# VectorE's finishing of a group, moved one slot later and put between the sum and the cast of h

## What is computed

```python
h = x                                            # relu(layernorm(x)) of the layer
for l in range(5):
    m = jnp.einsum('bnd,de->bne', h, weight[l])
    agg = jnp.einsum('bij,bid->bjd', A, m)       # A = (adj != 0)
    gi, gh = agg @ w_ih.T + b_ih, h @ w_hh.T + b_hh
    r = sigmoid(gi_r + gh_r)
    z = sigmoid(gi_z + gh_z)
    n = tanh(gi_n + r * gh_n)
    h = (1 - z) * n + z * h
out = x + h * mask[..., None]
```

## Time and profile before

| | |
|---|---|
| median of 3 runs | 686.35 us (685.84 to 688.16) |
| the profiled execution's own time | 686.79 us |
| its span, first to last instruction | 684.7 us |
| busy: PE / DVE / ACT / POOL | 95% / 87% / 77% / 60% of the span |
| gated layer, first slots | from about 300 us |
| gated layer, finishing inside the rounds | 420 to 660 us |

### The profile page before, as it was taken

How to read it: one execution, slowest core, us unless ns; L and a number is a source line. 1 busy time by engine, 2 the same in 40 slices (tenths; PEclk the granted TensorE clock), 3 DMA queues, 4 the chain that set the end, 5 groups by cost and what they waited for, 6 DMA issues and landing times. The chain is left out here.

```text
span 684.7 us, 13204 instructions
## 1 busy us (share of the span) xinstructions
PE 652.9 (95%) x4380; PEld 424.8 (62%) x4380; DVE 594.9 (87%) x1349; ACT 526.3 (77%) x964; POOL 410.2 (60%) x367
## 2 busy tenths in 40 slices
PE   4899999999999999989999999999999999999995
PEld 3678888888888888865555444545555555555452
DVE  3877787777778877888999899999999999999995
ACT  3688888888888888867687787777877777877774
POOL 4556676677666666464774755555555555555554
PEclk9999999999999999999999999999999999999997
DMA  6111111111000110012232333333333343333532
GB/s 159 32 33 32 32 32 32 32 32 34 22 19 24 32 32 17 10 24 47 51 59 49 59 63 74 67 78 70 69 62 65 76 79 77 61 64 78 78 74 66
DMA packets 114691, 35.82 MB, mean 52 GB/s; under 512 B 87681, under 2 KB 114625, under 8 KB 114625
## 3 DMA queue, kind: packets, MB, share of 16 engines
q1 hardware_dynamic: 113424, 34.79, 23.9%
q10 hardware_dynamic: 1200, 0.20, 0.2%
HBM read 9.80 MB, written 4.19 MB: 20 GB/s over the span
## 5 line engine op out<-in xcount | busy, mean ns | idle before, releaser
L1553 POOL TENSOR_TENSOR h0T<-r,zh 128x512 f32<-128x512 f32 x80 | 104.1, 1302 | 140.4 <-DVE r L1587 140.2
L52 PE MATMUL psum<-t_parts,gru_w 128*128 128x512 f16 x720 | 181.7, 379 | 6.2 <-DVE t_parts L1577 6.2
L52 PE MATMUL psum<-h_parts,gru_w 128*128 128x512 f16 x720 | 181.8, 379 | 2.1 <-DVE r L1591 1.2
L52 PEld LDWEIGHTS psum<-h_parts,gru_w 128*128 128x128 f16 x720 | 69.7, 98 | 83.6 <-DVE r L1591 5.3
L52 PEld LDWEIGHTS psum<-t_parts,gru_w 128*128 128x128 f16 x720 | 65.4, 98 | 77.0 <-DVE t_parts L1577 15.5
L1547 POOL TENSOR_TENSOR zh<-z,h0T 128x512 f32<-128x512 f32 x80 | 102.7, 1284 | 15.0 <-ACT z L1525 14.7
L1522 ACT CAST t_parts<-psum 128x512 f16<-128x512 f32 x80 | 46.8, 585 | 60.9 <-PE psum L52 60.6
L1435 DVE CAST h_parts<-h0T 128x512 f16<-128x512 f32 x80 | 84.0, 1050 | 2.0 <-POOL h0T L1553 1.9
L691 POOL TENSOR_TENSOR prob<-prob,row_max 128x512 f32<-128x512 f32 x64 | 68.7, 1086 | 22.3 <-DVE row_max L1179 21.5
L1530 ACT ACTIVATE r<-r,gates_b 128x512 f32<-128x512 f32 x80 | 64.9, 812 | 17.5 <-DVE r L1581 17.2
L1525 ACT ACTIVATE z<-psum,gates_b 128x512 f32<-128x512 f32 x80 | 62.3, 778 | 5.8 <-PE psum L52 0.9
(11 more groups left out here) (135 smaller groups left out, 1199.4 us busy)
## 6 DMA issues: line engine op xcount, KB each, us to landing
x_all<-in_x SPq DMA_DIRECT2D x16, 256.0 KB, 3.3
adj<-in_adj SPq DMA_DIRECT2D x16, 256.0 KB, 2.9
out_x<-y SPq DMA_DIRECT2D x14, 256.0 KB, 2.3
h_nodes<-h_parts SPq DMA_TRANSPOSE x80, 3.0
out_x<-zT SPq DMA_DIRECT2D x2, 256.0 KB, 2.3
gw<-in_L_gnn_weight SPq DMA_DIRECT2D x1, 320.0 KB, 6.5
W<-in_L_gnn_W SPq DMA_DIRECT2D x2, 128.0 KB, 2.6
wi<-in_L_gnn_w_ih SPq DMA_DIRECT2D x1, 192.0 KB, 7.4
```

What stands on the lines that cost most here:

```text
L52: return nc.tensor.matmul(out, lhsT, rhs, start=start, stop=stop)
L1553: pool.tensor_tensor(state(now), by_graph(r[now.s][:, :]), by_graph(zh[now.s][:, :]), ALU.add)\
```

## The change

`finish` of a group that ends inside the rounds is done one slot later on DVE, and no longer at the slot's end but after the sum (L1581) and ahead of the cast (L1435). `remaining(j)` moves to the same place in its own slot. The finishing of the last four groups stays where it was. SP's store of a group is issued one slot later too, behind that slot's DMA transpose. PE, ACT and POOL keep their order; no instruction is added or taken away.

```diff
+    def ended_at(j):
+
+        p, i, s = j // SLOTS, j % SLOTS // STREAMS, j % STREAMS
+        return Ended(p, i, 0) if 0 < p < ROUNDS and i > 0 and s == 1 else None
+
+    def ended_before(j, back):
+        return ended_at(j - back)
...
                 v.tensor_tensor(r[two.s][:, :], two.T, r[two.s][:, :], ALU.add).then_inc(summed, 1)
+            if ended_before(j, 1):
+                finish(ended_before(j, 1))
+            remaining(j)
             if now and j > 1:
                 state_parts(dve, now)
...
-            if ended is not None:
+            if ended is not None and ended.count > GROUPS - STREAMS:
                 finish(ended)
-            remaining(j)
...
             if at(0):
                 turn(at(0))
-            if ended is not None:
+            if ended_before(j, 1):
+                store(ended_before(j, 1))
+            if ended is not None and ended.count > GROUPS - STREAMS:
                 store(ended)
```

More of the change, by code:

```diff
@@ L1418, in slots @@
                 for s in range(STREAMS):
-                    one_slot(p, i, s, Ended(p, i, 0) if p > 0 and i > 0 and s == 1 else None)
+                    one_slot(p, i, s, ended_at(p * SLOTS + i * STREAMS + s))
         for s in range(STREAMS):
```

## The result

| | median, us | range of the runs | span of the profiled execution |
|---|---|---|---|
| before | 686.1 | 684.95 to 688.16 | 684.7 |
| after | 679.01 | 678.75 to 679.44 | 676.6 |

The change makes the kernel faster: the ratio is 0.9892, with a 95% interval of 0.9879 to 0.9905, about 7.1 us less. The forecast was 681.1 us.

A forecast was written before the change was run, and what follows sets the result against it. PE was taken as the bound, stalled by DVE's `t_parts` at twelve finishings. 686.79 - 4.8 (finishings) - 0.5 (first slots) = 681.5 us, or 681.1 against the median; range 679.3 to 684.3.

The forecast's parts named there:

- the finishing: Twelve finishings inside the rounds: moved ahead of the cast, they fill its wait for POOL and PE's stalls go, 4.8 us.
- The second rival: Finishing in its new place waits for POOL's `zh`, so the kernel gets slower, 690 us; chance 0.03.
- the first rival: In finishing slots `zh` comes later and PE waits for the gate instead of `t_parts`: 683.5 to 685.9 us; chance 0.12.
- the transposes: DMA transposes with a store right behind: land in 3.0 us, PE needs them after 4.1 to 4.3, cost 0.
- so 0.5 us survive of 1.2: `remaining(j)` of slots 2 to 14: about 1.0 to 1.2 us gained at slot 15, 0.5 left after slot 17.
- Slots 2 to 7: First steps of `remaining(j)`: 0.2 us lost in slot 2, slot 6's 0.3 given back in slot 7.
- where DVE is the slower one either way: Slot 7: DVE paces it with or without the move, so slot 6's 0.3 us is given back there.
- The loss of 0.2 in slot 2: Slot 2: the moved shift waits for POOL's `rstd`, so the gate ends about 311.5 while PE wants it at 311.38.
- a delay that is given back: Slot 6: the cast waits 0.3 us behind the added output, which slot 7 gives back.
- Slot 10: Shift of slot 10, moved ahead of the cast: of PE's 0.60 us wait at slot 11, 0.2 is left.
- Slot 14: Moments of slot 14, moved ahead of the cast: of PE's 1.13 us at slot 15, 0.3 is left.
- Slot 17: PE's gate wait behind POOL's normalising of group 15: POOL's mix comes only 0.5 us earlier, so part of the gain goes.

The follow-up runs named there:

- e1: Against the kernel after, `remaining(j)` stays at the slot's end, so only the finishing and its store move; 682.0 us.
- e4: Against the kernel after, the finishing stands between the remainder and the mix, behind the cast, still one slot later; 689.93 us.
- e8: Against the kernel after, POOL's normalising of groups 14 and 15 is cut in two, the multiplication one slot later; 678.74 us.
- e5: Against the kernel after, two of the four 128x128 instructions are done again in each of the twelve finishings; 685.65 us.
- e11: Against the kernel after, the moments of slot 7 are put back at the slot's end; single run, 681.46 us.
- e9: Against the kernel after, the shift and scaled weights of slot 2 are put back at its end; single run, 681.22 us.
- e10: Against the kernel after, the adding of an output in slot 6 is put back at its end; single run, 679.6 us.
- e12: Against the kernel after, the moments of slot 14 are put back at the slot's end; single run, 679.52 us.
- e3: Against the kernel after, the finishing is done one slot later too, but at that slot's end, ahead of `t_parts`; 689.17 us.

## Why the prediction was right in one term and short in the other

**Right: the finishing.** It rested on three steps, and each came out. The stalls in twelve slots go (5.21 became 4.77 in slot 45). They were not 0.44 each, as the prediction read from that one slot, but 0.40 on average; its 4.8 came from the sum over all slots, and stands. The finishing runs beside `zh` at 341 ns an instruction. The cast behind it takes 0.42. 4.8 us were forecast; by PE's starts e1 and the profile after have 4.8 (e1's median has 4.6). From slot 25 to 78 the prediction worked out 234.9 us without the stalls, and PE took 234.95, 0.14 of it in a longer slot 43 that no row explains.

The second rival asked whether the mask counts as a second SBUF input. It does not here: all 48 instructions took 341 ns on average, with `zh` beside them. The Trainium skill ("SBUF — State Buffer", § Who interferes with whom) says that DVE takes the pair that it shares with GpSimd for casts in their fast mode and, to read, with two SBUF inputs; the trace agrees at three places: the cast (0.42 alone, 1.34 beside `zh` in e4), the remainder (0.69, and 1.65 in e8), and the finishing (unchanged).

**Right with less room than thought: the first rival.** The gate is 0.17 us ahead of need in slot 26, and e5 puts what is left at 0.1. I had laid the slot out from rows of before in which PE was late: they put `t_parts` 1.23 us ahead of PE's start of slot 26 (422.27 and 423.50), and it lay 1.12 ahead (419.58 and 420.70). It did not tip, but it was nearer than the rival's room of 0.4 us said.

**Right: the transposes.** 3.1 us, and a store 0.2 us longer; nobody waits, though the room was 3.9 us and not over 4.

**Wrong: "so 0.5 us survive of 1.2".** This is the step that failed. The first slots gave 1.80, and the 1.3 between them lie here:

- *Slots 2 to 7: forecast a loss of 0.2, measured a gain of 0.61 at slot 8.* It is 0.8 of the 1.3. The prediction read two waits for `t_parts`, at slots 11 and 15, and missed a third of the same kind behind the moments of slot 7. The row of before was there to be read:

```profile
339.14 1.47 PE L52 MATMUL psum<-t_parts,gru_w 128*128 128x512 f16 x6 [0.67 <-DVE t_parts L1577]
```

  I had passed slot 7 over with "where DVE is the slower one either way". e11 measures it: 0.78 us. The loss of 0.2 in slot 2 did not come as forecast: e9, which puts it back, is level with the kernel after up to slot 7, 0.20 us ahead at slot 8 and 0.07 from slot 11 on. I had taken POOL's root (L714) at the 1.33 us of the earlier trace rows; in the kernel after no cast lies beside it and it took 1.03, the gate ended at 310.30 and PE's n part, due at 309.81 + 0.65 = 310.46, never waited. Slot 6 gives 0.15 (e10) where I had a delay that is given back.
- *Slot 10: forecast 0.40, measured 0.57.* The shift still takes 1.08 us ahead of the cast; with the 0.41 of the cast that is 1.42 for both (346.83 to 348.25), hardly more than a normal cast alone (1.25).
- *Slot 14: forecast 0.83, measured 0.92* between slots 11 and 15; e12 has 0.85.
- *Slot 17: forecast 0.5 to 0.7 given back, measured 0.30, and 0.61 to 0.64 in e3, e4 and e5.* That PE waits here for the gate behind POOL's normalising was right (1.47 us). POOL reached that work earlier than I had it: the root's first instruction starts at 374.85, 68.97 behind slot 2's start, against 377.14, 70.34 behind, before; that is 1.4 us and I had 0.5.

The 0.30 belongs to slot 14's moments: with these alone put back, 0.85 at slot 15 become 0.56 at slot 18 (e12), as 2.10 become 1.80 before. The other 0.3 is POOL's power beside the cast, which the same code shows at either length. So the prediction's loss at slot 17 was about right for e3 to e5, and that the profiled execution had the small one is luck, worth 0.3 us. In e11 and in e3 POOL's power and subtraction took 1.32 and 1.37 us, in the kernel after 1.02 and 1.11. How often an execution falls on either side is not known, since each kernel has one profile, and what decides it by some hundredths of a microsecond was not varied by itself.

**The range.** Its lower end, 679.3, stood for the best case of the first slots, and the kernel came 0.3 below it. By the prediction's own bound of 2.0 us more it should have been 681.1 - 2.0 = 679.1, which the kernel passed by 0.1. With the 6.6 us of the change's own, the forecast from 686.35 would have been 679.75. The other 0.7 is the median of before (686.35 in the first three runs, 686.1 in six) and scatter. A mechanism that works twelve times was carried over with full weight; the same mechanism in the first slots was discounted to less than half for three worries: slots 2 and 6, which came to a loss of 0.07 and a gain of 0.15, and slot 17, which took 0.3 of the gain here and 0.6 where the same code met the longer power. And the one step that gave most of the difference, slot 7, was not priced at all.

## What to carry to other kernels

When one engine's instruction waits for another engine's access to SBUF, its slot holds a stretch in which nothing is done. Find it by holding the same instruction's durations against each other (0.42 and 1.25 us here), and put work there that does not wait for the same thing. Two conditions met here: the work no longer stood ahead of what PE needed (e3), and it stood ahead of the instruction that waits (e4; two instructions further on, the same work cost 11 us more).

Such a hole is worth its own length and no more. Here 1.03 us of work filled one of 0.83, and half as much again gave nearly all of the gain back (e5). Check the room that is left before adding.

For a step that is moved in many places, make one table of all waits that it causes, and price every one by the same rule; the single steps can be read to 0.1 us from starts counted from a common point, even where the whole time scatters by 2 us. Check that on kernels with the same code first: behind slot 17 here they differ by 0.3 us.

## What the runs showed of the hardware

- POOL's 128x4 power (L714) took 1.31 to 1.33 us in all 18 places of the thirteen profiles where a DVE cast started 0.01 to 0.04 us behind it, and 1.02 or 1.03 in the 34 others: with no cast beside it (305.62 in the kernel after), with one that started 0.47 to 0.49 behind, and in five places with one that started 0.04 or 0.05 behind (375.14 in the kernel after; 0.04 is found on both sides). The cast took 0.41 to 0.43 in each of them. So a cast can run beside this instruction, and a few hundredths of a microsecond decide what that costs POOL.
- A DVE instruction on 128x4 with two SBUF tensors took 0.15 us alone, and 0.95 and 1.08 us beside POOL (and 346.83 after): its price here was the wait for POOL's instruction, not its own work.
- The stretch ahead of the first L1199 took 30.8 to 32.9 us in the thirteen profiles, though its code is the same in all of them. How much of the scatter of the runs' times this is can't be said, since only one execution of each kernel is profiled; why it varies was not looked into.
